# Values made with weights stationary and turned on PE, in the first stage of an adaLN attention block

## The reference, cut to what matters

```python
mod = (silu(c) @ wmod).reshape(4, 6, 1, -1)          # shifts, scales and gates, one set per sequence
h = layernorm(x) * (1 + ca) + sa
q = h @ wq_w + wq_b                                  # 1024 columns
k = h @ wk_w + wk_b                                  # 256 columns
v = h @ wv_w + wv_b                                  # 256 columns
x = x + ga * attention(q, k, v)
...                                                  # then a gated low-rank layer on a second layernorm
```

## Time and profile before

| | us |
|---|---|
| median of 3 runs | 3176.2 (3172.26 to 3180.29) |
| profiled execution | 3167.2 |
| its span in the trace | 3165.4 |
| `project` in the span, to the first load of `attend` | 0 to 657.9 |

### The profile page before, as it was taken

One profiled execution on the slowest core, in us unless ns is written; L12 is line 12 of the kernel. 1 busy time (PEld: TensorE's weight loads), 2 busy tenths in 40 slices (PEclk: granted clock), 3 DMA queues, 4 the chain that ended last, 5 costly groups with the idle time before them and its releaser, 6 DMA issues. The chain is left out here.

```text
span 3165.4 us, 49778 instructions
## 1 busy us (share of the span) xinstructions
PE 3014.9 (95%) x15590; PEld 1742.8 (55%) x15590; DVE 1960.9 (62%) x2572; ACT 1566.5 (49%) x2906; POOL 1796.5 (57%) x595
## 2 busy tenths in 40 slices
PE   5899999979999999999999999999999987999997
PEld 3788888844444444444444444444444435777776
DVE  4433343257767777777677677677777735666665
ACT  2111111126666666666666666666666662444444
POOL 2333333247777778778778778777787784211110
PEclk9899999979999999999999999999999998999999
DMA  6433434241122121121221221221211104333331
GB/s 228 163 135 130 147 118 154 98 132 46 35 53 48 35 52 43 40 53 36 46 52 34 49 52 34 49 50 37 49 43 43 39 11 157 100 100 99 97 96 67
DMA packets 156453, 241.46 MB, mean 76 GB/s; under 512 B 48992, under 2 KB 90400, under 8 KB 156320
## 3 DMA queue, kind: packets, MB, share of 16 engines
q1 hardware_dynamic: 156320, 240.05, 26.2%
HBM read 159.12 MB, written 79.82 MB: 75 GB/s over the span
## 5 line engine op out<-in xcount | busy, mean ns | idle before, releaser
L853 DVE TENSOR_REDUCE mx<-s_ps 128x1 f32<-128x1024 f32 x1024 | 1234.0, 1224 | 530.6 <-PE s_ps L926 527.8
L833 ACT ACTIVATE p_t<-st_ps 128x512 f32<-128x512 f32 x2048 | 1174.4, 598 | 708.5 <-PE st_ps L951 586.7
L791 POOL TENSOR_TENSOR p_sum<-p_sum,p_t 128x2048 f32<-128x2048 f32 x256 | 1171.6, 4577 | 22.1
L951 PE MATMUL st_ps<-q_st,k_st 98*128 98x512 f32 x2048 | 918.8, 454 | 24.2 <-ACT p_t L833 17.8
L951 PEld LDWEIGHTS st_ps<-q_st,k_st 98*128 98x128 f32 x2048 | 382.2, 187 | 753.7 <-ACT p_t L833 529.3
L926 PE MATMUL s_ps<-k_st,q_st 96*128 96x512 f32 x2048 | 658.7, 403 | 14.8 <-DMA q_st<-q_hi_d 11.1
L965 PE MATMUL num_ps<-p_t,v_sb 128*32 128x512 f32 x4096 | 545.5, 605 | 0.9 <-ACT p_t L833 0.9
L791 POOL TENSOR_TENSOR p_sum<-p_t 128x2048 f32<-128x2048 f32 x64 | 293.2, 4581 | 429.2 <-ACT p_t L833 429.2
L926 PEld LDWEIGHTS s_ps<-k_st,q_st 96*128 96x128 f32 x2048 | 389.1, 192 | 74.0 <-DVE mx L853 15.5
L372 POOL TENSOR_TENSOR o_lo<-side,o_hi 128x512 fp32r<-128x512 f32 x80 | 104.7, 1309 | 340.7 <-ACT o_hi L342 340.7
L1220 POOL TENSOR_TENSOR a_lo<-a_f,a_hi 128x1024 fp32r<-128x1024 f32 x32 | 76.2, 2382 | 389.0 <-ACT a_hi L1255 388.9
(11 more groups left out here) (129 smaller groups left out, 2812.8 us busy)
## 6 DMA issues: line engine op xcount, KB each, us to landing
q_st<-q_hi_d SPq DMA_DIRECT2D x128, 256.0 KB, 4.4
stage<-w_mod SPq DMA_DIRECT2D x48, 512.0 KB, 5.5
q_hi_d<-o_hi SPq DMA_DIRECT2D x64, 256.0 KB, 2.0
q_lo_d<-o_lo SPq DMA_DIRECT2D x64, 256.0 KB, 2.0
q_st<-q_lo_d SPq DMA_DIRECT2D x64, 256.0 KB, 4.2
att_d<-a_sb SPq DMA_DIRECT2D x128, 128.0 KB, 2.3
a_f<-att_d SPq DMA_DIRECT2D x32, 512.0 KB, 4.7
x_sb<-x SPq DMA_DIRECT2D x32, 512.0 KB, 5.4
```

Of the source, the lines that this page charges most:

```text
L791: nc.gpsimd.tensor_tensor(total, before, p_t[:, kt, :, :], ALU.add).then_inc(sum_done, 1)
L833: nc.scalar.activation(p_t[:, s, c, :], st_ps[:, c % 2, :], ACT.Exp, scale=SCALE)\
L853: nc.vector.tensor_reduce(mx[:, slot % 2, e:e + 1], s_ps[:, e % 2, :], AX_X, ALU.max)\
L951: nc.tensor.matmul(st_ps[:, c % 2, :], k_st[:, slot // 2, s * P:(s + 1) * P], q_st[:, slot, jj, h * QW:(h + 1) * QW], start=True, stop=True)\
```

## The change

The values are made as q and k are: 2 groups of 24 matmuls with a weight piece stationary and 512 tokens moving, in place of 4 groups of 24 with 256 columns moving. A block has 12 groups in the order q (0 to 7), v (8, 9), k (10, 11). DVE evicts a v group into `o_f` with the bias. A new event "vturn" stands behind groups 9 and 10: PE transposes the four 128x128 pieces of the v group before into a new PSUM bank `v_ps`, ACT copies that, reordered, into `v_f`, and SP sends it in one DMA of 512 B runs per partition, where four DMAs with 128 B runs stood. The bias of v is loaded as two columns instead of 256 values broadcast to all partitions. In `PREPARE` all entries of the second half after its fetch move one group up: stats to 6, norm to 7, turns to 8, 9, 10 and 11. `MODULATE` is as it was, with "mod 1" behind group 11.

```diff
-    QG, KG, VG = KT, KVT, BLK // P
-    NG = QG + KG + VG
+    QG, VG, KG = KT, KVT, KVT
+    NG = QG + VG + KG
     QK = QG + KG
+    NT = BLK // P
...
-               5: [("turn", 0, 6), ("turn", 0, 7), ("fetch", 1)], 7: [("stats", 1)], 8: [("norm", 1)],
-               9: [("turn", 1, 0), ("turn", 1, 1)], 10: [("turn", 1, 2), ("turn", 1, 3)],
-               11: [("turn", 1, 4), ("turn", 1, 5)], 12: [("turn", 1, 6), ("turn", 1, 7)]}
+               5: [("turn", 0, 6), ("turn", 0, 7), ("fetch", 1)], 6: [("stats", 1)], 7: [("norm", 1)],
+               8: [("turn", 1, 0), ("turn", 1, 1)], 9: [("turn", 1, 2), ("turn", 1, 3)],
+               10: [("turn", 1, 4), ("turn", 1, 5)], 11: [("turn", 1, 6), ("turn", 1, 7)]}
+
+
+    VTURN = {QG + 1 + v: [("vturn", v)] for v in range(VG)}
...
+    def kind(g):
+
+        return "q" if g < QG else ("v" if g < QG + VG else "k")
+
+    def split_index(g):
+
+        return g if g < QG else g - VG
...
+            seen += VTURN.get(g, [])
...
+        v_ps = ctx.enter_context(nc.psum_tensor("v_ps", [P, 512], F32))
...
-                sp.dma_start(bias_v[:, :], b_v.partition_broadcast(P)).then_inc(small_in, 16)
+                for v in range(VG):
+                    sp.dma_start(bias_v[:, v:v + 1], b_v[v * P:(v + 1) * P].rearrange("(p o) -> p o", o=1))\
+                      .then_inc(small_in, 16)
...
-                        elif ev[0] == "group":
-                            v = ev[1] - QK
-                            sp.wait_ge(o_taken, i * NG + (ev[1] + 1))
-                            dst = v_d.rearrange("i p t c -> t p i c")[par * VG + v][:, bass.ds(b * G, G), :]
-                            sp.dma_start(dst, v_f[:, v % 2, :].rearrange("p (i c) -> p i c", c=HD))\
-                              .then_inc(v_out[v % 2], 16)
+                        elif ev[0] == "vturn":
+                            v = ev[1]
+                            sp.wait_ge(v_taken, i * VG + (v + 1))
+                            dst = v_d.rearrange("i p t c -> p i t c")[:, bass.ds(b * G + v * (P // HD), P // HD),
+                                                                     par * NT:(par + 1) * NT, :]
+                            sp.dma_start(dst, v_f.rearrange("p (i t c) -> p i t c", t=NT, c=HD)).then_inc(v_out, 16)
...
+                        elif ev[0] == "vturn":
+                            v = ev[1]
+                            act.wait_ge(v_turned, i * VG + (v + 1))
+
+                            act.wait_ge(v_out, i * (16 * VG) + 16 * v)
+                            nc.scalar.copy(v_f.rearrange("p (i t c) -> p t i c", t=NT, c=HD),
+                                           v_ps[:, :].rearrange("p (t i c) -> p t i c", t=NT, c=HD)).then_inc(v_taken, 1)
 
...
-                            if g < QK:
-                                if not (is_int(i, 0) and g < 2):
-
-                                    dve.wait_ge(o_lo_done, i * QK + (g - 1))
-                                nc.vector.tensor_scalar(o_f[:, g % 2, :], o_ps[:, bank, :], bias_qk[:, g:g + 1],
-                                                        None, ALU.add).then_inc(o_taken, 1)
-                            else:
-                                v = g - QK
-
-                                dve.wait_ge(v_out[v % 2], i * (16 * VG // 2) + 16 * (v // 2))
-                                nc.vector.tensor_tensor(v_f[:, v % 2, :], o_ps[:, bank, 0:NKV], bias_v[:, :],
-                                                        ALU.add).then_inc(o_taken, 1)
+
+                            if kind(g - 2) == "v":
+                                dve.wait_ge(v_turned, i * VG + (g - 2 - QG + 1))
+                            elif not (is_int(i, 0) and g < 2):
+                                dve.wait_ge(o_lo_done, i * QK + (split_index(g - 2) + 1 if g >= 2 else g - 1))
+                            bias = bias_v[:, g - QG:g - QG + 1] if kind(g) == "v" else \
+                                bias_qk[:, split_index(g):split_index(g) + 1]
+                            nc.vector.tensor_scalar(o_f[:, g % 2, :], o_ps[:, bank, :], bias, None, ALU.add)\
+                              .then_inc(o_taken, 1)
...
+                            at = {"q": g, "v": g + KG, "k": g - VG}[kind(g)] * P
                             for kt in range(KT):
                                 for n, (h, w) in enumerate(((h_hi, w_hi), (h_hi, w_lo), (h_lo, w_hi))):
                                     begin, end = kt == 0 and n == 0, kt == KT - 1 and n == 2
-                                    if g < QK:
-                                        last = nc.tensor.matmul(o_ps[:, bank, :], w[:, kt, g * P:(g + 1) * P],
-                                                                h[:, par, kt, :], start=begin, stop=end)
-                                    else:
-                                        v = g - QK
-                                        last = nc.tensor.matmul(o_ps[:, bank, 0:NKV],
-                                                                h[:, par, kt, v * P:(v + 1) * P],
-                                                                w[:, kt, D + NKV:NW], start=begin, stop=end)
+                                    last = nc.tensor.matmul(o_ps[:, bank, :], w[:, kt, at:at + P],
+                                                            h[:, par, kt, :], start=begin, stop=end)
                             last.then_inc(o_ready, 1)
+                        elif ev[0] == "vturn":
+                            v = ev[1]
+                            pe.wait_ge(o_taken, i * NG + (QG + v + 1))
+                            if not (is_int(i, 0) and v == 0):
+                                pe.wait_ge(v_taken, i * VG + v)
+                            for t in range(NT):
+                                last = nc.tensor.transpose(v_ps[:, t * P:(t + 1) * P],
+                                                           o_f[:, (QG + v) % 2, t * P:(t + 1) * P], ident[:, :])
+                            last.then_inc(v_turned, 1)
```

More of the change, by code:

```diff
@@ L157, in project @@
         bias_qk = sb("bias_qk", [P, QK], F32)
-        bias_v = sb("bias_v", [P, NKV], F32)
+        bias_v = sb("bias_v", [P, VG], F32)
         stats = sb("stats", [P, HT, 2, 6], F32)
@@ L164, in project @@
         o_f = side[:, 0:2 * BLK].rearrange("p (u s) -> p u s", u=2)
-        v_f = side[:, 2 * BLK:3 * BLK].rearrange("p (u n) -> p u n", u=2)
+        v_f = side[:, 2 * BLK:3 * BLK]
         mrow, mmax, mmin, mgate = (side[:, 3 * BLK + n * HALF:3 * BLK + (n + 1) * HALF] for n in range(4))
@@ L197, in project @@
         qk_out = [sem(f"qk_out{s}") for s in range(2)]
-        v_out = [sem(f"v_out{s}") for s in range(2)]
+        v_turned = sem("v_turned")
+        v_taken = sem("v_taken")
+        v_out = sem("v_out")
         row_ready = sem("row_ready")
@@ L261, in do @@
                             fetch(i * 2 + (2 + ev[1]))
-                        elif ev[0] == "group" and ev[1] < QK:
+                        elif ev[0] == "group" and kind(ev[1]) != "v":
                             g = ev[1]
+                            n = split_index(g)
                             if g < QG:
@@ L269, in do @@
                                 dst_hi, dst_lo = k_hi_d, k_lo_d
[L270 to L271 removed]
+                                rows = bass.ds(b * (G * HD) + (g - QG - VG) * P, P)
+                            sp.wait_ge(o_hi_done, i * QK + (n + 1))
                             sp.dma_start(dst_hi[rows, cols], o_hi[:, g % 2, :].bitcast(F32)).then_inc(qk_out[g % 2], 16)
[L273 removed]
+                            sp.wait_ge(o_lo_done, i * QK + (n + 1))
                             sp.dma_start(dst_lo[rows, cols], o_lo[:, g % 2, :].bitcast(F32)).then_inc(qk_out[g % 2], 16)
[L275 to L280 removed]
+                        elif ev[0] == "vturn":
[4 more added lines that the diff above has]
+                            sp.dma_start(dst, v_f.rearrange("p (i t c) -> p i t c", t=NT, c=HD)).then_inc(v_out, 16)
                         elif ev[0] == "rows":
@@ L302, in _ @@
                     sp.wait_ge(qk_out[s], 32 * NBLK * QK // 2)
-                    sp.wait_ge(v_out[s], 16 * NBLK * VG // 2)
+                sp.wait_ge(v_out, 16 * NBLK * VG)
                 sp.wait_ge(row_out, 16 * 8 * NB)
@@ L307, in _ @@
             def _(act):
-                act.wait_ge(small_in, 80)
+                act.wait_ge(small_in, 64 + 16 * VG)
                 nc.scalar.activation(ce[:, :, :], cs[:, :, :], ACT.Exp, scale=-1.0).then_inc(c_exp, 1)
@@ L336, in do @@
                               .then_inc(h_hi_done, 1)
-                        elif ev[0] == "group" and ev[1] < QK:
+                        elif ev[0] == "group" and kind(ev[1]) != "v":
                             g = ev[1]
                             act.wait_ge(o_taken, i * NG + (g + 1))
-                            act.wait_ge(qk_out[g % 2], i * (32 * QK // 2) + 32 * (g // 2))
+                            act.wait_ge(qk_out[g % 2], i * (32 * QK // 2) + 32 * (split_index(g) // 2))
```

(6 more changed lines are left out.)

## The result

The changed kernel takes 3239.7 us (median of 4 runs, 3237.2 to 3246.2) against 3174.2 for the kernel before on the same chip (4 runs, 3169.5 to 3180.3): ratio 1.0211, interval 1.0195 to 1.0227. That is slower, as forecast, but by 65 us and not by 37, and outside the range of 3193 to 3228. Between the two profiled executions the span grows from 3165.4 to 3237.2 us, by 71.8.

The account below looks back on a forecast made before the run. PE's matmul stream was taken to bound the kernel. The terms -5.1 + 7.7 + 28.9 + 14.7 - 12.0 + 2.3 = +36.5 us, added to the median 3176.2, gave 3213 us, range 3193 to 3228.

Parts of the forecast that it names:

- signs of being wrong: In `project`: seam wait under 1 us, seam wait grown by something queued ahead of `h_lo`, or x waits staying in addition.
- values: matmuls and transposes, 8 blocks: PE's v groups in `project`: wide matmuls save 5.1 us, added transposes cost 7.7, together +2.6 us.
- seam waits: Between blocks, group 0 waits for all sixteen `h_lo`: 4.3 us behind four modulating blocks, 3.9 behind three plain, +28.9 us.
- clock behind seams: PE's matmuls after each of seven seams run at a reduced granted clock: 2.1 us each, +14.7 us, bounds 0 to 19.
- x waits given back: Waits for normalized x in blocks 2, 4, 6 and their clock cost, 13.0 us, shrink to about 1: -12.0 us.
- end of the stage: End of `project`: last group is now k, whose `o_lo` and DMA delay the first load of `attend`, +2.3 us.
- The matmuls: PE in `project`: two wide groups replace four narrow ones, saving 0.64 us per block, 5.1 us over 8 blocks.
- The edits at nothing: In `project`: ACT's `v_ps` copy (0.6 us), DVE evictions, bias loads (start moves well under 0.5 us), earlier stats and norm: 0.
- the clock stays up: Rival, seams of `project`: no clock loss, so 14.7 us go and x is late by 1.3: +25, 3201; chance 0.14.
- no wait, with 1.6 us to spare: Behind modulating blocks, x can be turned at E + 21.3 and PE arrives at E + 22.9 (E: preceding group's eviction).
- The seam costs nothing: Rival, between blocks: the turns' chain is done before PE asks, x waits as before: 3181; chance 0.05.
- The other side, faster: Rival, SP's queue: fewer value DMAs bring x in time, 13.0 us go, seam covered too: -8.1, 3168; chance 0.03.

Follow-up runs that it names:

- b_act20: Kernel before, with 20 more instructions on ACT that only count a semaphore, ahead of its first weight cast: 3204.5 us (1 run).
- b_dve236: Kernel before, with 236 more instructions on DVE that only count a semaphore, ahead of its wait for the modulation matmuls: 3196.6 us (1 run).
- a_back: Changed kernel, with 236 counting instructions more on ACT and 20 more on DVE, restoring their later programs' places in a block of 256: 3204.3 us, ratio 1.0091.
- b_act256: Kernel before, with 256 counting instructions more on ACT and 256 more on DVE: 3185.3 us (1 run).
- b_act180: Kernel before, with 180 counting instructions more on ACT alone: 3169.3 us.
- a_split: Changed kernel, with group 0 of a block waiting slice by slice for the late `h_lo` tiles instead of all sixteen at once: 3233.3 us (1 run).
- b_first: Kernel before, with the next block's first half of x fetched ahead of the four gate-weight loads in SP's queue: 3157.5 us, ratio 0.9955.
- a_best: Changed kernel with slice-wise `h_lo` wait, x fetched ahead of gate weights and gate-row DMAs, 236 counting instructions on ACT and 20 on DVE: 3160.0 us, ratio 0.9969.

## Why the prediction was right and wrong

**The step that failed** is its first: "the change lies in `project`, so only that stage is read further". 38 of the 71.8 us lie in `attend` (+26.9) and `finish` (+11.1). Their code, data and DMAs are the same; their instructions on ACT and DVE lie 20 further on and 20 further back. `b_act20` and `b_dve236` make the two costs singly in the kernel before (+28.7 and +11.3), `a_back` removes 35.6 of the 38 from the changed one, and `b_act256` shows that 256 instructions are no displacement. No rival of the prediction had this mechanism, and none of its signs of being wrong appeared, since all of them look at `project`. Its trace of before could have suggested it: the restarts of `attend` took 30.7 us where other pairs took 29.7, and ACT waited 2.7 us at each, put down to POOL's `p_sum`. A wait that comes at restarts only points to the loop, whatever releaser is named; in `b_act180` it went with the place of ACT's code. Nor did the sum ask what a change of instruction counts (two fewer groups in each of the unrolled blocks, a new event on ACT) does to loops that come later.

**The sum for `project`, by its terms**, +33.8 measured against +36.5:

| term | forecast | measured | from |
|---|---|---|---|
| values: matmuls and transposes, 8 blocks | -5.1 + 7.7 | +2.6 | block 7 behind its first eviction: 60.47 before, 60.80 after, 8 x 0.33 |
| seam waits | +28.9 | +29.2 | waits row, 7 times |
| clock behind seams | +14.7 | +16.4 | gaps, after against `a_split` |
| x waits given back | -12.0 | -13.0 | 8.8 of waits, none left in blocks 2, 4, 6; 4.2 of clock as read from before |
| end of the stage | +2.3 | +2.1 | last eviction to first load, 5.30 against 3.17 |
| block 0 | 0 | -2.2 | group 4 evicted at 98.73 instead of 100.93 |

These add up to 35.1; 1.3 us of difference to 33.8 are not assigned. The last row cannot be put down to the change: group 4 of block 0 is evicted at 98.73 to 100.44 in the five kernels with twelve groups and at 100.18 to 100.93 in the five with fourteen where DVE counts nothing, so within each kind it differs from kernel to kernel. That the stage came out 2.7 us below its forecast is therefore in large part chance.

*The matmuls.* Right, with the price of the kernel's own pairs of load and matmul. The formula of the Trainium skill, "TensorE: Matmul & The Clock Gate", section Back-to-back issue gap, which the prediction weighed against it, would have given the values -1.0 + 7.7 = 6.7 us; 2.6 were measured. The section states that formula for a matmul in isolation, and a group here is a stream of pairs, so it was not the figure to hold against the rows.

*The edits at nothing.* Right for the copy from `v_ps`: the source view of after has 16 of them at 579 to 587 ns, so the reordering in runs of 32 costs nothing over a plain cast, and PE never waits for it. The start moved by less than the 0.5 us forecast: the first eviction is at 71.86 instead of 72.28.

*The seam.* Right in place, releaser and size. To read how long the turns' chain takes at a place where the trace of before has the same chain in another position gave 4.3 and 3.9 us per seam, and after has 29.2 us for the seven.

*The clock.* Right in kind and near in size: 16.4 / 7 = 2.3 us for each seam, where the mean of two rows gave 2.1. In the first 4 us of group 0 of block 2 (223.3 to 227.3) the windows view of after has the clock at 0.57, and in the stretch from 225 on, over the end of the slow matmuls, at 0.76:

```profile
225.00:229.00 4.00, 4.00 (x15) 3.25 (x14) 0.00 (x0) 0.00 (x0) 0.00 (x0) 0.76 1.01 396
```

The rival that the clock stays up falls with it.

*x.* The waits of blocks 2, 4 and 6 went as worked out. But "no wait, with 1.6 us to spare" was read as a gift of the seams, and `a_split` shows it to be a coincidence of two delays: without the seam waits PE would wait 25 us for x, in six blocks instead of three. `b_first` and `a_best` put the cause in what SP sends ahead of x: with the fetch sent first, the same x is never late. Whether the loads ahead of it hold x up in the queue or by taking bandwidth, these runs do not tell apart.

*The rivals.* "The seam costs nothing" falls with its 29.2 us. "The other side, faster" falls as well: removing the x waits moved the end of `project` by 11.3 us in `b_first` (with one restart of PE against it), near the 13.0 priced, but the change itself did it only by being late elsewhere.

## What to carry to other kernels

An edit in one stage moves the code of all later ones, so a prediction or a comparison should look at every loop behind it: compare the distance over a loop's restart with that inside it on each engine, look for `issue` waits at the first instructions of a loop, and, where a loop is as long as the two here (342 and 362 instructions), try some counting instructions ahead of it before blaming the edit. Put them where the engine has time, and look at the earlier stages too: `b_act180` gained 12.2 us in `attend` and lost as much in `project`. A wait that comes only at restarts belongs to the restart even where the profile names another engine. Price a seam by the chain that must run in it, read where the same chain stands elsewhere in the trace, and add the clock behind it. Before removing a wait, ask which other delay runs beside it, and change both in one run.

## What the runs showed of the hardware

The cost of a loop's restart depends on where the loop lies. For ACT's loop of 342 instructions in `attend` a restart cost 30.7 - 29.7 = 1.0 us at the place of the kernel before, 3.0 us at 20 instructions further on, and nothing measurable at 180 further on (29.7); 256 further on it was as before. For DVE's loop of 362 instructions in `finish` two restarts cost 11 us together at 20 back (6 in `a_split`), and less than 1 at the place of before. Less than half of the price shows as ACT's `issue`: it waits 11.6 us and the stage loses 26.9, part of it on PE, whose eight `num_ps` matmuls take 1.94 instead of 1.07 us at a granted clock of 0.55.

The reordering copy from PSUM on ACT, with its input read in runs of 32 elements, takes 0.58 us for 128 x 512, no more than the plain cast of the same size at 0.62.
